# A causal mask moved from TensorE's accumulation to a fused add-and-maximum on VectorE

## What is computed

```python
scores = jnp.einsum('bhqd,bhkd->bhqk', qh, kh) * inv_sqrt_d
causal = jnp.tril(jnp.ones((sq, sk), dtype=bool))
scores = jnp.where(causal, scores, jnp.finfo(scores.dtype).min)
attn = jax.nn.softmax(scores, axis=-1)
out = jnp.einsum('bhqk,bhkd->bhqd', attn, vh)
```

## Time and profile before

| | |
|---|---|
| Time, median of 3 runs | 1180.89 us (1178.44 to 1182.04) |
| Profiled execution | 1178.57 us, span 1176.8 us |
| TensorE (PE) busy | 1138.1 us, 97% of the span |
| TensorE weight loads (PEld) busy | 770.9 us, 66% |
| VectorE (DVE) busy | 670.4 us, 57% |
| ScalarE (ACT) busy | 485.4 us, 41% |
| GpSimd (POOL) busy | 432.8 us, 37% |
| Reductions for maxima (L1290) | 432 operations, 282.3 us |
| Granted TensorE clock | full |

### The profile page before, as it was taken

One profiled execution on the slowest core, in us unless ns is written; L12 is line 12 of the kernel. 1 busy time (PEld: TensorE's weight loads), 2 busy tenths in 40 slices (PEclk: granted clock), 3 DMA queues, 4 the chain that ended last, 5 costly groups with the idle time before them and its releaser, 6 DMA issues.

```text
span 1176.8 us, 15866 instructions
## 1 busy us (share of the span) xinstructions
PE 1138.1 (97%) x6016; PEld 770.9 (66%) x6016; DVE 670.4 (57%) x966; ACT 485.4 (41%) x792; POOL 432.8 (37%) x398
## 2 busy tenths in 40 slices
PE   5999999999999999999999999999999999999998
PEld 4745666656656554666666666557887887887886
DVE  5776767677676667667668667654534224134212
ACT  4365454456545655645635545552321111111110
POOL 1256534443556765344454556663101001001000
PEclk9999999999999999999999999999999999999999
DMA  6933433333334444435345445411310000000000
GB/s 233 285 103 91 115 124 83 95 108 90 91 103 143 118 126 127 138 107 163 109 124 141 137 126 171 116 46 38 97 54 36 1 1 36 0 0 29 7 1 36
DMA packets 73735, 110.30 MB, mean 94 GB/s; under 512 B 6976, under 2 KB 45888, under 8 KB 71744
## 3 DMA queue, kind: packets, MB, share of 16 engines
q1 hardware_dynamic: 70864, 102.00, 29.2%
q0 software_dynamic: 2080, 6.82, 2.1%
q10 hardware_dynamic: 720, 0.54, 0.1%
HBM read 71.58 MB, written 37.75 MB: 93 GB/s over the span
## 4 chain that ended last, share of the span: by engine, by line
PE 88%; ACT 4%; DVE 2%; issue 2%; POOL 2%; DMA 1%; SPq 0%; DVEq 0%; ACTq 0%; POOLq 0%
PE PS L951 18%; PE PS L952 17%; PE PS L953 17%; PE PS L1084 11%; PE PS L1069 10%; PE PS L1047 9%; ACT PT L870 1%; PE PS L965 1%; PE PS L1050 1%; PE PS L1072 1%; ACT stackQ L855 1%; PE PS L1079 1%; POOL P_sum L734 1%; DVE m_cols L1290 1%; DMA stackK<-scratch 1%
## 5 line engine op out<-in xcount | busy, mean ns | idle before, releaser
L1290 DVE TENSOR_REDUCE m_cols<-PS 128x1 f32<-128x512 f32 (+3 forms) x432 | 282.3, 668 | 150.4 <-PE PS L1047 75.7
L870 ACT ACTIVATE PT<-PS 128x512 f32<-128x512 f32 (+1 forms) x432 | 238.8, 581 | 189.7 <-PE PS L1069 76.5
L734 POOL TENSOR_TENSOR P_sum<-PT 128x512 f32<-128x512 f32 x128 | 161.7, 1283 | 306.1 <-ACT PT L870 306.1
L1069 PE MATMUL PS<-stackQ,stackK 100*128 100x512 f32 (+3 forms) x512 | 182.1, 403 | 12.3 <-ACT PT L870 12.0
L1047 PE MATMUL PS<-stackK,stackQ 96*128 96x512 f32 (+3 forms) x512 | 179.0, 386 | 2.5 <-DVE m_cols L1290 1.3
L923 ACT ACTIVATE hid<-PS,b1c 128x512 f32<-128x512 f32 x64 | 44.1, 690 | 279.7 <-PE PS L953 277.7
L1371 DVE CAST hidH<-hid 128x512 fp32r<-128x512 f32 x64 | 28.8, 451 | 224.6 <-ACT hid L923 221.9
L1069 PEld LDWEIGHTS PS<-stackQ,stackK 100*128 100x128 f32 x512 | 90.7, 190 | 88.3 <-ACT PT L870 40.1
L1298 DVE RECIPROCAL P_sum<-PS 128x512 f32<-128x512 f32 x32 | 107.4, 3358 | 42.9 <-PE PS L1084 42.9
L1047 PEld LDWEIGHTS PS<-stackK,stackQ 96*128 96x128 f32 x512 | 91.9, 190 | 51.7 <-DVE m_cols L1290 23.1
L740 POOL TENSOR_TENSOR P_sum<-P_sum,PT 128x512 f32<-128x512 f32 x96 | 120.8, 1284 | 8.8 <-ACT PT L870 4.6
(11 more groups left out here) (124 smaller groups left out, 1782.0 us busy)
## 6 DMA issues: line engine op xcount, KB each, us to landing
scratch<-stage SPq DMA_DIRECT2D x128, 256.0 KB, 2.5
stackK<-scratch SPq DMA_DIRECT2D x62, 256.0 KB, 4.0
stackQ<-scratch SPq DMA_DIRECT2D x46, 256.0 KB, 3.9
stackQ<-scratch SPq DMA_DIRECT2D x18, 512.0 KB, 4.8
stackK<-scratch SPq DMA_DIRECT2D x60, 128.0 KB, 4.4
stackQ<-scratch SPq DMA_DIRECT2D x28, 128.0 KB, 3.7
PT<-wT SPq DMA_DIRECT2D x3, 1024.0 KB, 8.7
x_res<-x SPq DMA_DIRECT2D x3, 1024.0 KB, 9.3
```

The costliest lines, as they stand in the source:

```text
L734: pool.tensor_tensor(P_sum[:, h, :], PT[:, h, :], PT[:, 4 + h, :], ALU.add).then_inc(p_added, 1)
L870: nc.scalar.activation(PT[:, slot:slot + heads, q0:SEQ], PS[:, T_BANK + n % 2, 0:heads * width].rearrange("p (h n) -> p h n", h=heads), AC ...
L1069: mm = nc.tensor.matmul(dst[:, a, :], stackK[0:STACK + HPG, par, h + a, k * P:(k + 1) * P], stackQ[0:STACK + HPG, par, h + a, q0:SEQ], sta ...
L1290: nc.vector.tensor_reduce(m_cols[:, q, STACK + h:STACK + h + heads], PS[:, S_BANK + m % 2, 0:heads * n].rearrange("p (h n) -> p h n", h=he ...
```

## The change

The mask tile becomes float32 and 128 x 512: zeros, with the same triangle in its last 128 columns. The last n columns of it are the mask for a query tile with n keys. `scores_for_max` no longer adds the mask for cross units. VectorE's `maximum` does it instead: for a cross unit it issues one `tensor_tensor_reduce` for each head of the fill, which adds the mask to the scores, writes the sums back to the bank and gives their maximum. Self units keep their single `tensor_reduce`. The first use waits for the constants. To make room for the larger tile, the scratch for GpSimd's DMA descriptors is halved.

```diff
+LOWEST = -3e38
...
-        mask_qk = sb("mask_qk", [P, P], BF16)
+        mask_qk = sb("mask_qk", [P, SEQ], F32)
...
-            pool.affine_select(out=mask_qk[:, :], in_=mask_qk[:, :], compare_op=ALU.is_ge, fill=MASKED,
+            pool.affine_select(out=mask_qk[:, SEQ - P:SEQ], in_=mask_qk[:, SEQ - P:SEQ], compare_op=ALU.is_ge, fill=MASKED,
                                base=0, pattern=[[-1, P]], channel_multiplier=1).then_inc(consts, 1)
...
                 dst = PS[:, S_BANK + m % 2, 0:heads * n].rearrange("p (h n) -> p h n", h=heads)
-                cross = layer_of(u) == CROSS
                 for a in range(heads):
                     mm = nc.tensor.matmul(dst[:, a, :], stackQ[0:STACK, par, h + a, q * P:(q + 1) * P],
-                                          stackK[0:STACK, par, h + a, 0:n], start=a == 0, stop=not cross)
-                if cross:
-                    mm = nc.tensor.matmul(dst[:, :, n - P:n], identb[:, :],
-                                          mask_qk[:, :].unsqueeze(1).broadcast_to([P, heads, P]), start=False, stop=True)
+                                          stackK[0:STACK, par, h + a, 0:n], start=a == 0, stop=a == heads - 1)
                 mm.then_inc(s_full, 1)
...
                 dve.wait_ge(s_full, m + 1)
-                nc.vector.tensor_reduce(m_cols[:, q, STACK + h:STACK + h + heads],
-                                        PS[:, S_BANK + m % 2, 0:heads * n].rearrange("p (h n) -> p h n", h=heads),
-                                        AX.X, ALU.max).then_inc(s_done, 1)
+                bank = PS[:, S_BANK + m % 2, 0:heads * n].rearrange("p (h n) -> p h n", h=heads)
+                if layer_of(u) == SELF:
+                    nc.vector.tensor_reduce(m_cols[:, q, STACK + h:STACK + h + heads], bank, AX.X, ALU.max).then_inc(s_done, 1)
+                else:
+                    if u == FIRST_CROSS and i == 0:
+                        dve.wait_ge(consts, CONSTS)
+
+                    for a in range(heads):
+                        top = nc.vector.tensor_tensor_reduce(bank[:, a, :], bank[:, a, :], mask_qk[:, SEQ - n:SEQ], 1.0, LOWEST,
+                                                             ALU.add, ALU.max, m_cols[:, q, STACK + h + a:STACK + h + a + 1])
+                    top.then_inc(s_done, 1)
...
-    nc = bacc.Bacc("TRN2", target_bir_lowering=False, num_devices=1, dynamic_dma_scratch_size=4096)
+    nc = bacc.Bacc("TRN2", target_bir_lowering=False, num_devices=1, dynamic_dma_scratch_size=2048)
```

## The result

The changed kernel takes 1168.49 us (median of 4, 1166.16 to 1170.79) against 1179.99 us for the kernel before in the same session: ratio 0.990, interval 0.9882 to 0.9918, 11.5 us less. The forecast was faster with 0.70, 1163 us in 1155 to 1184; the direction and the range hold, the gain was forecast half as large again.

The account below looks back on a forecast made before the run. The prediction took TensorE as the bound: 24.8 us removed, less 5.6 of stalls and 1 of late VectorE work, gives 18.2 us, so 1163 us against the median of 1180.89; range 1155 to 1184.

Parts of the forecast that it names:

- TensorE as the bound, VectorE with room: Cross stage: TensorE busy 320.5 of 327 us; VectorE idle 6.3 us a unit, against 1.4 us added.
- What is removed from TensorE: Cross-unit maxima: 176 mask matmuls on TensorE go, 1.55 us a unit, 24.8 us in all; bounds 16 and 45.
- The 0.13 us for every mask: Mask matmuls of 128 columns, from spacings of starts with and without a mask; the same taken for 256 columns.
- the 0.25 us for 512 columns: The one 512-column mask matmul in each cross unit: 0.12 us more than the 0.13 for 128 columns.
- the low bound: Least gain on TensorE: the masking matmuls' share of the stage's chain, 4.7% of 343 us, 16 us.
- e = 0.07: VectorE, cross maxima: extra us of each fused operation beyond a plain reduction, 16 a unit; bounds zero and 0.155.
- the second rival: VectorE's fused operations each pay their whole 155 ns, so nothing is gained: 1181 us, chance 0.10.
- the third rival: VectorE's fused operations run at half rate, from same-bank PSUM access or the custom program: 1220 us; everything slower 0.20.
- Where TensorE then waits: Score banks, cross stage: TensorE stalls for VectorE's maxima, 0.8 us in each of 4 units, 0.2 in 12: 5.6 us.
- The 1 us for late V copies and residual adds: VectorE work queued behind longer maxima releases general banks and stores late: 1 us over the stage, 0 to 3.
- At nothing: Priced at zero: the larger mask memset, VectorE's wait on the constants, the halved scratch for GpSimd's DMA descriptors.
- The first rival: VectorE's accumulator is dearer, e about 0.11 to 0.14, costing 7 to 8 us at 0.12: 1171 us, chance 0.15.

Follow-up runs that it names:

- The alignment: No run: traces of the kernel before and the changed kernel laid upon each other, comparing matmul starts around each of 176 masks; 0.09 us each on average, 16.4 us.
- the kernel without masks: Kernel before with no mask added for cross maxima on either engine, VectorE taking the plain maximum: 1164.17 us, ratio 0.9864 to the kernel before.

## Why the prediction was right in sign and too large

**TensorE as the bound, VectorE with room: right.** VectorE's busy time in a batch was forecast at about 63 us and is 62.3; the prediction's own 1.4 us a unit would have made 64, and it is 0.95. The batch was forecast at 79 and is 80.9.

**"What is removed from TensorE", 24.8 us: the step that failed.** The mechanism was right, the size was not. The alignment gives 16.4 us in the changed kernel, and the kernel without masks gains 14.8 by its median. There were two errors. The 0.13 us for every mask came from masks in front of a projection, the neighbour that makes them dearest. There it is nearly right (0.118 on average); the same place in the changed kernel:

```profile
654.53 0.39 PE L1047 MATMUL PS<-stackK,stackQ 96*128 96x512 f32 x1
654.76 0.40 PE L952 MATMUL PS<-WH,oTH 128*128 128x512 f32 x1
654.99 0.40 PE L953 MATMUL PS<-WL,oTH 128*128 128x512 f32 x1
```

0.46 us from the first to the third, where the earlier trace rows have 0.60. But 105 of the 176 masks stand in front of something else and are worth 0.05 to 0.09. And the 0.25 us for 512 columns came from one place, at 641.93, in which the scores behind the mask did not follow at once: they started 0.15 us after it, where the matmul behind a mask of 128 columns follows after 0.04. That place before, then in the changed kernel:

```profile
641.46 0.64 PE L1047 MATMUL PS<-stackK,stackQ 96*128 96x128 f32 x4
641.93 0.39 PE L1050 MATMUL PS<-mask_qk,identb 128*128 128x512 bf16 x1
642.08 0.48 PE L1069 MATMUL PS<-stackQ,stackK 100*128 100x512 f32 x1
642.40 0.23 PE L1072 MATMUL PS<-mask_kq,identb 128*128 128x128 bf16 x1
...
635.88 0.64 PE L1047 MATMUL PS<-stackK,stackQ 96*128 96x128 f32 x4
636.50 0.47 PE L1066 MATMUL PS<-stackQ,stackK 100*128 100x512 f32 x1
636.81 0.23 PE L1069 MATMUL PS<-mask_kq,identb 128*128 128x128 bf16 x1
```

From the four scores matmuls to the next scores it is 0.62 us with the mask and without it, so that mask was worth nothing. The prediction had a number near the measured one in hand and called it the low bound: the chain's 4.7% of 343 us, 16 us. That it fits so well is luck in part. The chain gives 121 of the masks a flat 0.07 us, and it gives the mask at 641.93, which was worth nothing, 0.23.

**e = 0.07: a little high.** It is 0.03 to 0.05, in spite of an instruction of its own for the accumulator. The Trainium skill (VectorE: DVE Perf Modes, Two Vector instructions with no wait between them) says that an accumulator output is a second instruction; the trace agrees, with 256 rows of 142 ns. The estimate of 75 ns for it, by the Trainium skill (Vector Engine (DVE) Microarchitecture Reference, Measured stream behaviour on trn2), is higher than the 50 ns between starts that the accumulator and all else of the fused form cost together. The Trainium skill (VectorE: DVE Perf Modes, The TRN2 errata) says that many small tiles pay the latency of SBUF once each; here the mask comes from SBUF. The trace agrees in that a fixed part is there: 128 columns follow each other after 0.25 us, of which 0.14 are columns, so each tile pays 0.11. What this part is made of no run shows, and it is less than the 0.155 that the second rival needed. Reading and writing the same PSUM bank didn't slow them to half the rate, as the third rival had it: a column takes 1.07 ns against 1.04.

**Where TensorE then waits: right place, less than priced.** Forecast 5.6 + 1 = 6.6 us. The changed kernel against the one without masks loses 4.3 by the medians and 2.8 by the turns. The unit with the statistics was forecast to lose 0.8, and loses 0.7 (17.4 to 18.1), three times; the last self unit, with statistics too, loses 0.3 (21.6 to 21.9). The others were given 0.2 each, and lose 0.05 to 0.1. Part of the forecast waits may have fallen away because TensorE came less early than thought; that is argued, not shown. The 1 us for late V copies and residual adds was not measured apart.

**At nothing: right.** The scratch made no difference, and the first turn of the stage is at 447.4 to 448.1 us as before.

**The sum by its measured terms:** over the 15 stretches TensorE's part gives 13.8 us (321.13 to 307.37), the fused operations take 2.8, and some 11 are left. From turn to turn of the whole stage (447.58 to 785.44 before, 337.9 us) the second profile of the changed kernel has 326.1: 11.8, against 11.5 by the medians; the first, with the clock's fall, has 328.6. In the prediction two errors worked against each other, 8 to 10 us too much removed and 2 to 4 us too much waited, and so the forecast came nearer than its largest term deserved. That the time lies in the range is owed to the range's width as well.

**The rivals.** None came true. The first rival's time (1171) is nearest to 1168.5, but its mechanism, a dearer accumulator, is not the reason: e is smaller than forecast.

## What to carry to other kernels

A small matmul on a busy TensorE is worth what its neighbours leave of it, so price it from many places with different followers, and not from one clean spot. When work moves to an engine with idle time, look for the one unit in which that engine is already full: here VectorE's idle time in a batch, 25 us, was more than six times the 3.8 us of added work, and still one unit in four lost most of its gain. Work without a deadline, such as the statistics, can then be moved into a gap, where in front of another waiting piece of work it gives the gain back; and the whole stage has to be added up afterwards, since what one unit wins can be lost in a later one.

## What was not expected of the hardware

The fused add-and-maximum reads a bank of PSUM and writes it back at nearly the rate of a plain reduction: 707 - 570 = 137 ns for 128 columns, 1.07 ns each against 1.04. Its accumulator costs an instruction with a recorded 142 ns, but moves the next start by 50 ns or less. TensorE's clock fell to 0.50 for a few us in the midst of a stage in which TensorE is 97% busy, in one of the changed kernel's two profiles and not in the other, with no more than 0.65 us without a matmul in the 10 us ahead of it; the last stretch took 18.4 us with it and 15.9 without. The first unit of the last batch varies with the landing of the feed-forward weights: 25.2 to 25.7 us without the mask matmuls and with the statistics in place, 26.9 to 27.0 with them moved, and 25.3 to 26.6 with the mask matmuls.
